# Attention layer on one core: probabilities times values as three float32r products, a new order inside a pair of heads, low parts kept in memory

## The reference

```
att  = softmax(x, -1) / sqrt(1024);  adj = s (1024x1) * cond (1x1024) * att, diagonal -inf
x    = x + (1 where adj is among its 10240 largest elements, else 0)
scale, shift = split(cond @ W_emb + b_emb)
xn   = rms_norm(x, g_norm) * (1 + scale) + shift
q, k, v = heads of xn @ W_qkv;   q, k = rms_norm(q, g_q), rms_norm(k, g_k)
o    = softmax(q k^T / 8) v;     x = x + o + o @ W_out
```

## Time and profile before

| | |
|---|---|
| median of 3 runs | 3981.94 us (3981.88 to 3984.9) |
| the profiled execution | 3988.51 us, its span 3986.8 us |
| busy share | PE 94%, DVE 66%, ACT 39%, POOL 32% |
| mean granted clock of PE | 0.978 of full |

### The profile page before, as it was taken

How to read it: one execution, slowest core, us unless ns; L and a number is a source line. 1 busy time by engine, 2 the same in 40 slices (tenths; PEclk the granted TensorE clock), 3 DMA queues, 4 the chain that set the end, 5 groups by cost and what they waited for, 6 DMA issues and landing times.

```text
span 3986.8 us, 44387 instructions
## 1 busy us (share of the span) xinstructions
PE 3743.1 (94%) x16035; PEld 2436.3 (61%) x16035; DVE 2619.9 (66%) x4521; ACT 1537.1 (39%) x2724; POOL 1260.9 (32%) x1880
## 2 busy tenths in 40 slices
PE   5885899999998999999998999999998999999999
PEld 2333676666644766667644667667644667666644
DVE  8996677777787677777787677777787333233321
ACT  1004344444434344444434344444433244444430
POOL 2005433333315433333315433333314433333300
PEclk9997799999999999999999999999999999999999
DMA  4003000001025100000125100000033100000022
GB/s 159 0 5 116 17 22 22 22 22 37 22 91 192 34 22 22 22 22 22 33 96 184 42 22 22 22 22 22 22 107 132 47 22 22 22 22 22 22 81 88
DMA packets 165296, 193.68 MB, mean 49 GB/s; under 512 B 7336, under 2 KB 120032, under 8 KB 164064
## 3 DMA queue, kind: packets, MB, share of 16 engines
q1 hardware_dynamic: 165088, 190.98, 15.0%
HBM read 142.72 MB, written 48.23 MB: 48 GB/s over the span
## 4 chain that ended last, share of the span: by engine, by line
PE 73%; DVE 15%; ACT 4%; POOL 4%; issue 3%; DMA 1%; SPq 0%; DVEq 0%; ACTq 0%; POOLq 0%
PE pax L1209 23%; PE ppv L1278 19%; PE pst L1265 10%; PE pax L1245 7%; PE pst L1190 7%; DVE trash L797 3%; DVE xr L832 3%; DVE mx L985 3%; PE pax L1227 2%; POOL xn L419 2%; PE ppv L1209 2%; PE pax L1253 1%; ACT sA L666 1%; DMA pt<-out_x 1%; PE pst L1083 1%
## 5 line engine op out<-in xcount | busy, mean ns | idle before, releaser
L1209 PE MATMUL pax<-wh,xn 128*128 128x384 f32 x3840 | 1060.5, 347 | 21.9 <-POOL xn L419 21.9
L1278 PE MATMUL ppv<-pt,v 128*65 128x512 f32 x2048 | 990.9, 595 | 1.1 <-issue 1.1
L797 DVE TENSOR_SCALAR_CACHE_REDUCE trash<-keys,state 128x2048 uint8<-128x2048 f32 x384 | 900.1, 2344 | 9.8
L985 DVE TENSOR_REDUCE mx<-pax 128x1 f32<-128x512 f32 x960 | 618.6, 686 | 227.5 <-PE pax L1245 207.0
L1209 PEld LDWEIGHTS pax<-wh,xn 128*128 128x128 f32 x3840 | 704.9, 189 | 35.7 <-issue 35.7
L673 ACT ACTIVATE pt<-pst 128x1024 f32<-128x1024 f32 x512 | 524.0, 1023 | 506.2 <-PE pst L1265 447.9
L1209 PE MATMUL pax<-wl,xn 128*128 128x384 f32 x1920 | 649.1, 338 | 0.0
L971 DVE TENSOR_REDUCE ss<-sq 128x4 f32<-128x256 f32 x256 | 107.2, 419 | 759.8 <-ACT sq L648 759.8
L1245 PE MATMUL pax<-sA 65*128 65x512 f32 x960 | 466.0, 531 | 21.9 <-ACT sA L661 13.0
L1278 PEld LDWEIGHTS ppv<-pt,v 128*65 128x65 f32 x2048 | 278.8, 137 | 298.3 <-issue 224.6
L395 POOL TENSOR_TENSOR wl<-wf,wh 128x1024 fp32r<-128x1024 f32 x96 | 228.7, 2387 | 579.0 <-ACT wh L544 579.0
(11 more groups left out here) (144 smaller groups left out, 4574.6 us busy)
## 6 DMA issues: line engine op xcount, KB each, us to landing
wf<-in_L_cond_W_qkv SPq DMA_DIRECT2D x96, 512.0 KB, 5.4
keys<-in_x SPq DMA_DIRECT2D x32, 512.0 KB, 9.8
xin<-in_x SPq DMA_DIRECT2D x32, 512.0 KB, 4.0
out_x<-xin SPq DMA_DIRECT2D x32, 512.0 KB, 3.2
wo<-in_L_cond_W_out SPq DMA_DIRECT2D x4, 4096.0 KB, 13.5
pt<-out_x SPq DMA_DIRECT2D x64, 256.0 KB, 4.0
out_x<-pt SPq DMA_DIRECT2D x64, 256.0 KB, 2.1
oT_scr<-ostg SPq DMA_DIRECT2D x56, 256.0 KB, 2.0
```

Source lines behind the costliest of these rows:

```text
L797: e.tensor_scalar(trash[:], kv, thr_f, None, ALU.is_ge, ALU.add, accum_out=cnt[:, c:c + 1]).then_inc(z_cnt, 1)
L985: e.tensor_reduce(mx2[:, j // T, j % T, c:c + 1], max_banks(alone, j)[:, c, :], axis=AX, op=ALU.max).then_inc(m_mx, 1)
L1209: i = e.matmul(qkv_bank(alone, t)[:, 0:6 * DH], xn[:, a, k, t * P:(t + 1) * P], w[:, k, :, :].rearrange("p s c -> p (s c)"), start=(k == 0 ...
L1278: i = e.matmul(ppv[0:DH + 1, c, :], v2[:, par, kt, hh, :], pt[:, kt % 2, c * HALF:(c + 1) * HALF], start=(kt == 0), stop=(kt == T - 1))
```

## The change

- `values` becomes three float32r products, six matmuls for each `kt`: `vh`*`ph`, `vl`*`ph`, `vh`*`pl`. ACT computes each exp twice (`ph` rounded, `pf` full), POOL forms `pl` = `pf` - `ph` (new method `low`) for each of the 512 steps, and `vl` for each tile (one more POOL instruction in `prep_tile`). `ph`, `pf`, `pl` have three buffers.
- The order inside a pair is new on all engines. PE issues scores two steps ahead; the transposes of tile t+1 come after `prep_tile` t+2; `out_tokens` of both heads and `normalise` move to the start of the next pair; all of `score_max` lies in the steps 8 to 15. On DVE `prep_split` of tile t now stands between the two counts of the same t, where it was that of tile t-1, right behind `prep_sums` of t.
- To make room, the low part of the features is written to DRAM (`xl_scr`) and loaded tile by tile (`load_xl`, 512 KB for each tile of each pair, two buffers); the third product of `prep_tile` waits for it, the 16 matmuls ahead of it do not. High and low weights of the 8 pairs are split once, in batch 0, stored to DRAM (`keep_w`) and loaded by later batches as two 1.5 MB loads (`load_w`).
- Boundaries: one more projection ahead of the features, `prep_tile` 0 and 1 back to back, the sums of tile 0 ahead of the last `finalise_tile` on DVE.

```diff
 # Pool
+        def low(self, gp, hh, kt):
+            e, w = self.e, T * (2 * gp + hh) + kt
+            e.wait_ge(t_ex, CST + w + 1)
+            e.tensor_tensor(pl[:, w % 3, :], pf[:, w % 3, :], ph[:, w % 3, :].bitcast(F32),
+                            ALU.subtract).then_inc(t_lo, 1)
...
             e.tensor_copy(st[:, 0:2, 0:DH], qk[:, 0:2, :])
             e.tensor_copy(st[:, 2:4, DH:P], qk[:, 2:4, :]).then_inc(a_hi, 1)
+            e.wait_ge(a_v, u + 1)
+            e.tensor_tensor(vl[:, par, t, :, 0:DH], v, vh[:, par, t, :, 0:DH].bitcast(F32),
+                            ALU.subtract).then_inc(a_vs, 1)
...
+            for t in range(2, T):
                 if prep:
+                    self.prep_tile(gp + 1, t, 1 - par)
+                self.low(gp, (t + 1) // T, (t + 1) % T)
 # Vector, in pair()
             for t in range(T):
-                before = step_before(b, i, t) if search else None
                 if prep:
                     self.prep_sums(gp + 1, t)
-                    if t == T - 1:
-                        self.normalise(gp, 0)
-                    if t > 0:
-                        self.prep_split(gp + 1, t - 1)
-                    if before is not None:
-                        self.search_update(before)
-                    if search:
-                        self.search_count(z + t // 2, 2 * (t % 2))
-                    if t == T - 1:
-                        self.prep_split(gp + 1, t)
-                    if search:
-                        self.search_count(z + t // 2, 2 * (t % 2) + 1)
+                if t > 0 and before[t] is not None:
+                    self.search_update(before[t])
+                if search:
+                    self.search_count(z + t // 2, 2 * (t % 2))
+                if prep:
+                    self.prep_split(gp + 1, t)
+                if search:
+                    self.search_count(z + t // 2, 2 * (t % 2) + 1)
 # Tensor
         def values(self, gp, par, hh, kt, between=None):
...
+            e.wait_ge(t_eh, w + 1)
+            for m, v in enumerate((vh, vl)):
+                for c in range(2):
+                    e.matmul(ppv[0:DH + 1, c, :], v[:, par, kt, hh, :], ph[:, w % 3, c * HALF:(c + 1) * HALF],
+                             start=(kt == 0 and m == 0), stop=False, skip_group_check=True)
+            if between is not None:
+                between()
+            e.wait_ge(t_lo, CST + w + 1)
             for c in range(2):
-                i = e.matmul(ppv[0:DH + 1, c, :], v2[:, par, kt, hh, :], pt[:, kt % 2, c * HALF:(c + 1) * HALF],
-                             start=(kt == 0), stop=(kt == T - 1))
+                i = e.matmul(ppv[0:DH + 1, c, :], vh[:, par, kt, hh, :], pl[:, w % 3, c * HALF:(c + 1) * HALF],
+                             start=False, stop=(kt == T - 1), skip_group_check=True)
...
+            for t in range(2 * T):
+                gap = slots.get(t, [None] * 3)
+                if t + 2 < 2 * T:
+                    self.scores(gp, par, (t + 2) // T, (t + 2) % T)
+                fill(gap[0])
+                self.values(gp, par, t // T, t % T, lambda: fill(gap[1]))
                 if t == 0 and not first:
                     self.out_rows(gp - 1, 1)
+                    e.wait_ge(t_oe, 2 * gp)
+                if prep and t == 0:
+                    self.prep_tile(gp + 1, 1)
+                    self.transpose_tile(gp + 1, 0)
+                    self.prep_tile(gp + 1, 2, z=before[2])
+                if prep and t == 1:
+                    self.transpose_tile(gp + 1, 1)
+                if prep and 1 <= t <= T - 3:
+                    self.prep_tile(gp + 1, t + 2, z=before[t + 2])
+                    self.transpose_tile(gp + 1, t + 1)
 # Sync
+        def keep_w(self, n):
+            e = self.e
+            e.wait_ge(w_l, 3 * (n + 1))
+            e.dma_start(w_scr[n, :, 0, :], w_high.bitcast(F32)).then_inc(d_wst, 16)
+            e.dma_start(w_scr[n, :, 1, :], w_low.bitcast(F32)).then_inc(d_wst, 16)
+        def load_xl(self, gp, t):
+            e, u = self.e, T * gp + t
+            wait(e, a_qkv, u - 1)
+            e.dma_start(xl[:, u % 2].rearrange("p k c -> p (k c)").bitcast(F32), xl_scr[t]).then_inc(d_xl[u % 2], 16)
```

More of the change, by code:

```diff
@@ L724, in pair @@
-            self.out_move(gp, 1)
+            z = STEPS * b + 4 * i
+            before = [step_before(b, i, t) if search else None for t in range(T)]
+            new = b if first else None
+            self.exp(gp, 0, 0, new)
+            if before[0] is not None:
+                self.search_tot(before[0], 1)
+            self.max_row(gp, par, 1)
+            if prep:
+                self.prep_tile(gp + 1, 1 - par, 0)
+            self.exp(gp, 0, 1, new)
+            if not first:
+                self.out_rows(gp - 1, 0)
@@ new lines, in pair @@
+            self.exp(gp, 0, 2, new)
+            if not first:
+                self.out_rows(gp - 1, 1)
+            if prep:
+                self.prep_tile(gp + 1, 1 - par, 1)
+                self.stack_tile(gp + 1, 1 - par, 0)
+                self.prep_tile(gp + 1, 1 - par, 2, z=before[2])
+            self.exp(gp, 0, 3)
+            if prep:
+                self.stack_tile(gp + 1, 1 - par, 1)
+            for t in range(2, T - 1):
+                if prep:
+                    self.prep_tile(gp + 1, 1 - par, t + 1, z=before[t + 1])
+                    if t < T - 2:
+                        self.stack_tile(gp + 1, 1 - par, t)
+                self.exp(gp, (t + 2) // T, (t + 2) % T)
+                if search and not prep and t == 4:
+                    self.search_tot(z)
@@ new lines, in pair @@
+            if prep:
+                self.stack_tile(gp + 1, 1 - par, T - 2)
+            self.out_move(gp, 0, (PAIRS - 1) * b + i)
+            if prep:
+                self.stack_tile(gp + 1, 1 - par, T - 1)
+            self.exp(gp, 1, 1)
+            for t in range(T, 2 * T - 2):
+                self.exp(gp, 1, t + 2 - T)
+                if prep and gp + 2 < PAIRS and t in (8, 10, 12):
+                    self.split_w(gp + 2, (t - 8) // 2)
+                if search and not prep and t in (8, 12):
+                    self.search_tot(z + t // 4 - 1)
@@ L1240, in score_max @@
             for c in range(2):
[L1241 removed]
+                if j == T and alone or j and not alone:
                     e.wait_ge(m_mx, v + c - 1)
@@ L1306, in pair, with fill @@
             e, gp = self.e, PAIRS * b + i
+            z = STEPS * b + 4 * i
+            before = [step_before(b, i, t) if search else None for t in range(T)]
+            def fill(what):
+                if what == "row":
+                    e.wait_ge(t_ex, CST + T * (2 * gp + 2) - 1)
+                    self.max_row(gp + 1, 0)
+                elif what is not None:
+                    self.score_max(gp + 1, 1 - par, what)
+            slots = {8: [None, 0, 1], 9: [2, 3, None], 10: [4, 5, None], 11: [6, 7, None], 12: [8, 9, None],
+                     13: [10, 11, None], 14: [12, 13, "row"], 15: [14, 15, None]} if prep else {}
             if first and b > 0:
@@ L1368, in finish @@
+                fill(gap[2])
+                if search and not prep and t in (4, 8, 12):
+                    self.search_sum(z + t // 4 - 1)
         def finish(self):
```

551 lines of the change are left out of this document (300 added, 251 removed).

## The result

The changed kernel takes 4352.73 us (median of 4 runs, 4350.14 to 4353.23), the kernel before 3981.91 us in the same comparison: a ratio of 1.0928, 95% interval 1.0909 to 1.0947, so 9.3% slower. The forecast was 4310 us. The profiled execution took 4353.23 us, its span is 4351.4 us against 3986.8, or +364.6 us. Mean granted clock 0.931 against 0.978.

What follows compares the result with a forecast made beforehand. PE was taken to bound the kernel before, DVE's search loop the changed one. Terms: 3988.5 + 283 - 1 + 36 + 1 + 18 - 9 = 4316.5 us, less 6.6 to the median: 4310 us, range 3950 to 4380.

Steps and rivals of the forecast that it cites:

- With POOL next it is 4310: Behind POOL's last cast, vl and `low` go ahead of DVE's two splits, on both tiles: 4310 us, chance 0.46.
- the round: DVE's search loop over two tiles, which PE's search_sum of even tiles waits for: 19.2 us with both tiles colliding.
- rival 1: Only odd tiles collide, as the exp of t+1 comes after vl on even ones: 4178 us, chance 0.24.
- One sign: In the trace of pairs with search, PE idles ahead of L1369 for 3 to 5 us at each of three even tiles.
- rival 2: No collision of splits and `low`, since `low` finds its exp late or the splits win: 3965 us, faster, chance 0.16.
- Rival 3: PE stays the bound, needing DVE's two-tile time under 14.1 us and a short head: 3840 us, chance 0.06.
- xl behind `keep_w`: In batch 0, xl of tile 0 lands late behind the weight stores: +3 us, six times, +18 (0 to 40).
- Pairs without search: The split delays j = 0 by some 3 us, values take less: 93.5 us a pair, -1 in all.
- the sum: All terms added to the profiled time: 3988.5 + 283 - 1 + 36 + 1 + 18 - 9 = 4316.5 us.
- The three last pairs: Last pairs with search: four updates held up by `low` cost 14 us, less 2 for the earlier start: +12 each, +36.
- wait 1.2 and 2.3: In last pairs with search, an update's two-input instructions L812 and L817 wait 1.2 and 2.3 us for `low`.
- The four boundaries: Between batches, one projection (6.9 us) fills idle PE time, but tile 0's sums and keys come later: -9 us over four.

Runs made afterwards that it cites:

- e1_pool_waits: Changed kernel with POOL waiting for DVE's split of the tile before its vl subtraction and the `low` behind it: 4041 us, ratio 1.0133.
- e2_best: Changed kernel with POOL waiting for DVE's split, early xl loads for tiles 0 and 1, and PE's wait for ACT's second row copy later: 3973.31 us.
- e2_xl_early: Changed kernel with xl loads for tiles 0 and 1 ahead of the weight loads: batch 0 pairs 109.1 to 109.3 us instead of 112.6.
- e1_counts_first: Changed kernel with DVE's split moved behind both counts of its tile: 4068 us.
- e3_sums: Changed kernel with PE's search_sum in last pairs with search behind values 2, 7, 12 instead of 4, 8, 12: batch 1's last sum at 62.7 instead of 63.7 us.

## Why the prediction was right

**The step on which it rested.** "With POOL next it is 4310": the vl subtraction holds the first split (0.51 us; expected 0.5 to 0.8), `low` the second (2.46; 2.4 to 2.7), L494 stands right behind L603, and e1_pool_waits shows that this, with DVE's order left as it is, makes 13.5 of the 14.6 us by which the pair grew.

**The pair.** The search_sum that waits first comes 25.0 us into the pair at 1825.0 (predicted 26.0), the round is 19.3 (19.2), the first score_max stands at 83.6 (83.4), the second half takes 25.5 (24.6), the pair 109.1 (108.0). The round was right since both tiles collide: the even one, which I had put at 0.3 us from rival 1, collided as well (2.48 us at 1874.71). The second half is 0.9 us off: there the prediction took the earlier trace rows of another arrangement of the same matmuls less four values. One sign did not come as forecast: PE's idle time ahead of L1369 was put at 3 to 5 us at each of the three even tiles, and is 1.8, 3.6 and 2.6. PE's own work in these rounds is stretched instead: behind each of these waits its granted clock falls to 0.50, the lower of its two levels (1.2 GHz), for a few us (0.50 from 1870 to 1873 and from 1891 to 1894), and it is 1.00 in the head of the pair and in the second half. The prediction did not speak of the clock; the round came out all the same, since DVE sets it.

**Rivals.** Rival 1 needed L1125 at 0.28 us on even tiles and pairs of 101.7; rival 2 needed it everywhere. Neither occurred, but e1_pool_waits at 4041 is what rival 2 describes as a state, and it came out some 70 us above its 3965. Rival 3, PE as the bound, is seen in the pairs without search of e2_best (88.6 us; 93.7 less the 5.3 of the values is 88.4).

**Batch 0.** Predicted +18 for xl behind `keep_w`, measured 3.4 us in six pairs, 20, and 20.7 given back in these pairs by e2_xl_early.

**Pairs without search.** Predicted -1, measured -1.6.

**What was mis-sized.** The pairs with search gave +321.5 against the 283 + 18 = 301 of the sum. The three last pairs were put at +12 each; the ranks (DVE's step that closes the search) start 8.9, 10.6 and 9.3 us later behind the pair's first exp than before, 28.8 us in all. In place of "wait 1.2 and 2.3" in each of four updates, the updates took 3.6, 0.3 and 3.6 us more than before (1.3 in place of the last 3.6 in batch 2), and the one at the pair's start 1.5. The four boundaries were put at -9 and gave no such gain: behind the ranks the three between batches are 3.3 and 5.6 us longer and 8.2 shorter. Together that is the +29.4 of the table, close to the sum's 36 less 7 for three of the four boundaries, but by luck: the first term was 7 us too high, the second 7 too low. Last pairs, boundaries and the end are +38.4 together where the sum had 36 + 1 - 9 = 28, 8 of the difference in the last pair of batch 3 and the final projections (+9.0 for +1), and the start adds 6.5 that the sum did not have. Together 365 against 328, by these stretches nearly all of one sign: 37 of the 43 us between 4310 and 4353. The other 6 are the distance of the profiled execution of before from its median, which the sum took off and the changed kernel doesn't have (4353.23 against 4352.73).

**The length of the wait.** The Trainium skill, "SBUF — State Buffer", in the section on its two separate sides, says that whichever starts first, a GpSimd op that reads SBUF or a DVE op with two SBUF inputs, holds the shared ports for its whole length. The trace agrees: 2.46 us behind a `low` of 2.42, 1.38 behind a half of 1.3. It agrees in the order too wherever the second split waited in the changed kernel: there `low` had begun 0.11 us ahead of it. Where DVE's instruction was issued first and still passed (4.89 us, above), the rule does not say why. In e1_counts_first, with nothing ready on POOL, the second split ran at once.

## What to carry to other kernels

When work is added to POOL, list what DVE reads with two SBUF operands and look at who is ready behind POOL's current instruction: a 0.2 us instruction of DVE can cost one or two whole POOL instructions, and everything queued behind it on DVE is late by as much. If POOL has slack, let it wait for DVE's short instruction, one semaphore wait, rather than shorten or move things: here it took the ratio from 1.0928 to 1.0133. And a gain on the bounding engine is only collected once the engine that comes next is known; look for the round it must keep up with.

## What was not expected of the hardware

- DVE was passed twice in a row: 4.89 us for an instruction of 0.16, issued 0.1 to 0.2 us before the end of the second of four `low` (four in 9.46 us), which then waited for the third and the fourth. With `low` in halves DVE's split, issued 0.11 us behind the start of the first half, got in ahead of the second, 1.38 us. So POOL's next one does not always pass; what decides it is open. The double passing stands three times in e3_sums, once in each last pair (4.86 to 4.89 us).
- Copies under a predicate (L957, L958 in the changed kernel, L959 and L960 in e3_sums) read SBUF tiles too and took 0.20 to 0.21 us each time, in the middle of a `low` as well (2312.53), and DVE's counts, with one SBUF tile and one scalar, kept 2.33 to 2.35 us.
- PE's granted clock went down with its waits: 1.00 in a pair before, 0.92 in the changed kernel (0.50 for some us behind each wait for the counts, 1.00 otherwise), 0.98 to 1.00 in e1_pool_waits and e2_best. So part of what the waits cost stands in PE's busy time: 96.2 us in the pair against 89.0 in e2_best, with the same matmuls. Two stretches of 3 us behind such waits (columns as above):

```profile
1870.00:1873.00 3.00, 3.00 (x11) 2.11 (x11) 2.31 (x10) 2.88 (x8) 1.78 (x3) 0.50 0.00 0
...
1891.00:1894.00 3.00, 3.00 (x8) 1.70 (x7) 2.90 (x6) 2.56 (x4) 2.65 (x7) 0.50 0.00 0
```
